# Building the matrix of equal destinations from sign vectors in a two-stage graph network kernel

## The chip, the cores and the metric

The kernel runs as one program on one core of a Trainium2 chip. The metric is the device time of one launch in microseconds, the median of the timed runs. Engine names: PE is TensorE, DVE is VectorE, ACT is ScalarE, POOL is GpSimd, SP is SyncE.

## The reference, cut to what matters

The inputs are 100,000 nodes with 48 features and 25,000 edges, sorted by their destination. Stage one is a gated message pass that sums edge messages into the source nodes, stage two a relational message pass that sums into the destination nodes:

```
h1  = relu(einsum('ni,rij->nrj', h, weight1) + bias1)      # 8 relations
h2  = einsum('nrj,rjo->nro', h1, weight2)
msg = h2[src, rel_type] * norm
agg = segment_sum(msg, dst, num_segments=100000)
x   = x + relu(agg + bias2)
```

Here h is relu(layernorm(x)) after stage one.

## The kernel before

Edges are cut into 49 blocks of 512 (NBLOCK), each block into four tiles of 128 (TILES). Stage one runs over the 49 blocks, then stage two over ROUNDS = 53 rounds, then a closing pass streams 49 chunks of nodes through DVE to the output. All loops are unrolled in Python; each engine has one instruction list that it works through in order, and semaphores tie the lists together.

An indirect add to memory must not meet the same row twice in one transfer. So each block first sums the messages of equal destinations among its own edges: a matrix `same` holds, for tile t, a 1 where the destination of edge i in tiles 0 to t equals that of edge j in tile t and i is not later than j. Ten products per block (`sums_within`, lines 568 to 574) multiply its 128x128 parts with the messages; PE shows two records for each fp32 product. The row sums of `same` (`ahead1`) tell which edge is the last of its kind; `turned1` and `once1` make an index that sends all others to spare rows. POOL then adds four tiles of 128 rows to the table agg1 (`add1`, line 521), and gathers the rows of a block six ahead (`gather_wide`, line 512).

In stage two one round b of the engines' lists works on several blocks:

- DVE (lines 955 to 1063): asum and ac for the block a = b+1 that has just been gathered; v, y, yssq, yvar, yrstd, and three passes over v for x2 (960 elements wide, it also finishes 16 dense rows per partition); stat, cen, evar, erstd for e = b−1; and `same`, `turned1`, `once1` for d = b−2. `same_up_to` (line 854) compares the 512 keys of the block, which SP has broadcast to all 128 partitions (`load_rows1`, line 389), with the keys of one tile, multiplies by the mask `upto` and counts, in four instructions of 128, 256, 384 and 512 columns.
- ACT (lines 717 to 784): copies h2 transposed, scales msg1, squares and relus for block a, the three relus of the hidden layer (hid, 512 wide), the squares sq and ysq, the small square roots astd, estd and ystd, h2, the copy of the sums for POOL, and the copy of the second layer's result.
- PE (lines 620 to 663), for e = b−2 and f = b−3: transposes of h2 and of the messages, the first layer k0, k1, k2 in ps_k[0], ps_k[1], ps_k[0], the block's sums, and the second layer m1.
- POOL: four adds of block b, four gathers of block b+6. An add waits for ACT's copy of the sums and for once1.
- SP: the key rows, the kept values and the dense rows of the round, each after x2 of the round before.

The third set of first-layer products waits for ACT's first relu (line 645), and that stands on ACT behind the square and relu of ac (lines 734 to 742).

Of the kernel before, what the change touches and what calls it, by code (L numbers as in the profile page):

```python
# [7 lines left out]
I32 = mybir.dt.int32  # L8
BF16 = mybir.dt.bfloat16
# [56 lines left out]
POOL_SET = 15  # L66
CONSTS = 13

# [8 lines left out]
def build(nc, table, both, xt_in_dram, xn_in_dram, types, edge_src, edge_dst, src_rows, dst_rows, edge_feat, dist, norm, rel,  # L77
# [13 lines left out]
    with ExitStack() as ctx:  # L91
# [12 lines left out]
        ident = sb("ident", [P, P])  # L104
        iota_rel = sb("iota_rel", [P, NREL])
# [45 lines left out]
        sums1 = ring_of(sb, LAG1, "sums1", [P, TILES, H])  # L151
        junk_l = t2[0][:, :, :].rearrange("p r w -> p (r w)")
# [84 lines left out]
        def psum(name, shape):  # L237
# [14 lines left out]
        ps_h1 = ps_m[0:H, :]  # L252
        ps_gate = ps_s[:, BE // 2:BE // 2 + TILES * H]

        nodes_in = ring_of(sem, ARRIVE, "nodes_in")
# [23 lines left out]
                 "m1t_done msg1_done same1_done turned1_done once1_done sums1_done sums1_copied "  # L279
# [19 lines left out]
        def _(sp):  # L299
# [89 lines left out]
            def load_rows1(b):  # L389
                need(sp, S["same1_done"], b - 1)  # L390
                sp.dma_start(rows[b % 2][:, :], dst_rows[b:b + 1, :].to_broadcast([P, BE])).then_inc(rows_in[b % 2], 16)

            load_rows1(0)
            load_rows1(1)
            for i in range(SKEW, SKEW + T2S):
                load_wide(i)
            for i in range(ROUNDS):
                if 2 <= i < NBLOCK:
                    load_rows1(i)
                sp.wait_ge(S["x2_done"], i + 1)  # L400
                c, j = i - SKEW, i + T2S
                if 0 <= c < NBLOCK - RES:
                    sp.dma_start(x_mid[c], x2[c % 2][:, TILES:G, :].rearrange("p r w -> p (r w)")).then_inc(x_stored[c % 2], 16)
                if SKEW <= j < ROUNDS:
                    load_kept(j)
                    if j >= SKEW + T2S:
                        load_wide(j)
# [20 lines left out]
        def _(pool):  # L428
# [9 lines left out]
            def gather_tile(b, t):  # L438
                s = b % AHEAD
                c = b * TILES + t  # L440
                if t == 0:
# [8 lines left out]
                           allow_small_or_imprecise_dtypes=True).then_inc(S["pool_set"], 1)  # L450
            pool.wait_ge(S["idx_in"], 32)
# [85 lines left out]
        def _(pe):  # L537
# [81 lines left out]
            pe.wait_ge(S["rb1_in"], 2 * 16 * NREL)  # L619
            for b in range(2, NBLOCK + 3):  # L620
# [29 lines left out]
                if f >= 0:  # L650
                    pe.wait_ge(S["same1_done"], f + 1)
# [4 lines left out]
                if e < NBLOCK:  # L656
                    need(pe, S["m1_copied"], e)
# [5 lines left out]
                    last.then_inc(S["m1_done"], 1)  # L663

        @blk.scalar
        def _(act):
# [49 lines left out]

            for b in range(-1, ROUNDS):
# [58 lines left out]
                if 0 <= f < NBLOCK:  # L776
                    act.wait_ge(S["m1_done"], f + 1)
# [14 lines left out]
        def _(dve):  # L792
# [28 lines left out]
            dve.wait_ge(S["pool_set"], POOL_SET + 4)  # L821
            V.tensor_tensor(centre[:, :], centre[:, :], ident[0:2 * H, 0:2 * H], ALU.add).then_inc(S["vec_set"], 1)
# [132 lines left out]
            for b in range(-1, ROUNDS):  # L955
                a, e, d = b + 1, b - 1, b - 2
# [71 lines left out]
                if 0 <= d < NBLOCK:  # L1028
                    dve.wait_ge(S["same1_done"], d + 1)
# [113 lines left out]
```

## Time and profile before

| | us |
|---|---|
| median of 3 timed runs | 1540.43 (1537.09 to 1542.83) |
| span of the profiled execution | 1526.4 |
| stage two, roughly | 755 to 1415 of the span |
| closing pass | 1420 to the end |
| PE, PEld, DVE, ACT, POOL busy | 1130.4, 831.4, 1319.3, 668.1, 1026.1 |

The profile holds the span of the profiled execution, from its first to its last instruction, and no other time of it. Times in the trace count from the span's start. PE is the matmul stream, PEld the weight loads beside it. In a timeline a row merges instructions of one line, with their count behind the x; what stands in brackets is the idle time of the engine before the row and what ended it.

### The profile page before, as it was taken

The numbers are of one execution on the slowest core, as the hardware profiler recorded it, in microseconds if no ns is written. First come the engines' busy times: TensorE is split into PE (matmuls) and PEld (weight loads), VectorE is DVE, ScalarE is ACT, GpSimd is POOL, SyncE is SP. The second block draws the span as 40 slices with busy tenths as digits, with TensorE's granted clock in tenths as the row PEclk, the third lists the DMA queues.
The fourth block names the chain that finished last, engine by engine and source line by source line (L and its number), as shares of the span: only waits on it lengthen the run. The fifth ranks groups of instructions, "written<-read, shape, count | busy, mean of one in ns | idle before, by whom it ended". The sixth has DMA issues, their size and how long they took to land.

```text
span 1526.4 us, 20418 instructions
## 1 busy us (share of the span) xinstructions
PE 1130.4 (74%) x5198; PEld 831.4 (54%) x5198; DVE 1319.3 (86%) x3932; ACT 668.1 (44%) x1627; POOL 1026.1 (67%) x809
## 2 busy tenths in 40 slices
PE   5889899989999899881068888887878887775000
PEld 2767677777777777771035555555555555554000
DVE  6999999999989998980289999998989899888599
ACT  2444444544445444540155555555555555554000
POOL 7655667777877787566667787877777777766000
PEclk9666655655556655655575656655565556666555
DMA  7999986666666656642445666555555555554899
GB/s 225 307 324 327 328 236 157 153 146 143 142 166 149 149 139 143 155 101 11 100 120 143 166 167 156 140 138 137 136 139 127 132 131 138 138 127 81 328 400 398
DMA packets 154391, 268.73 MB, mean 176 GB/s; under 512 B 73818, under 2 KB 90411, under 8 KB 153380
## 3 DMA queue, kind: packets, MB, share of 16 engines
q1 hardware_dynamic: 78228, 223.53, 43.8%
q0 software_dynamic: 68992, 24.64, 18.5%
q10 hardware_dynamic: 7056, 19.27, 3.1%
q8 instruction: 43, 0.70, 0.2%
q14 instruction: 72, 0.59, 0.1%
HBM read 194.33 MB, written 112.55 MB: 201 GB/s over the span
## 4 chain that ended last, share of the span: by engine, by line
PE 34%; DVE 20%; DMA 19%; POOL 12%; issue 10%; ACT 3%; SPq 1%; POOLq 0%; DVEq 0%; ACTq 0%
PE ps_m L572 10%; POOL agg L485 8%; DMA t<-agg,src_all 6%; PE ps_m L661 6%; PE ps_qs L572 6%; DMA lows<-low 4%; PE ps_k L647 3%; DVE same L858 2%; DMA agg<-y,once 2%; DMA agg<-ysq,once 2%; DVE t L1074 2%; DVE x L1070 2%; PE ps_k L559 2%; PE ps_k L560 2%; PE ps_qs L610 1%
## 5 line engine op out<-in xcount | busy, mean ns | idle before, releaser
L521 POOL DMA_INDIRECT agg<-sums,once x196 | 312.7, 1595 | 103.5 <-issue 79.8
L443 POOL DMA_INDIRECT nodes<-in_table,dst_all x196 | 194.9, 995 | 102.2 <-issue 51.7
L512 POOL DMA_INDIRECT t<-agg,src_all x196 | 191.5, 977 | 66.1 <-issue 53.9
L572 PEld LDWEIGHTS ps_m<-msg,same 128*128 128x128 f32 x980 | 200.8, 314 | 29.0 <-issue 29.0
L572 PE MATMUL ps_m<-msg,same 128*128 128x48 f32 x980 | 208.5, 398 | 1.0 <-issue 1.0
L647 PE MATMUL ps_k<-h_t,rw_sb 56*128 56x256 f32 x588 | 122.7, 536 | 114.0 <-ACT hid L742 91.3
L572 PEld LDWEIGHTS ps_qs<-msg,same 128*128 128x128 f32 x980 | 183.6, 289 | 2.1 <-DVE msg L950 2.1
L572 PE MATMUL ps_qs<-msg,same 128*128 128x49 f32 x980 | 180.7, 363 | 2.0 <-DVE msg L950 2.0
L485 POOL DMA_INDIRECT agg<-x,once x84 | 137.4, 1635 | 43.9 <-issue 21.7
L647 PEld LDWEIGHTS ps_k<-h_t,rw_sb 56*128 56x128 f32 x588 | 62.9, 242 | 157.1 <-ACT hid L742 115.2
L559 PE MATMUL ps_k<-types_lo,low_hot 128*128 128x392 bf16 x196 | 95.7, 488 | 52.7 <-DVE low_hot L833 51.0
L661 PE MATMUL ps_m<-hid,rw_sb 128*64 128x256 f32 x588 | 133.8, 625 | 0.0
L973 DVE TENSOR_REDUCE asum<-t 128x4 f32<-128x192 f32 x49 | 17.1, 349 | 114.9 <-DMA t<-agg,src_all 114.8
L839 DVE SCALAR_TENSOR_TENSOR t<-iota_hi,hi_all,ps_k 128x392 f32<-128x392 f32 x196 | 113.8, 617 | 1.5 <-PE ps_k L560 1.5
L858 DVE SCALAR_TENSOR_TENSOR same<-rows,src_all,upto 128x128 f32<-128x128 int32 x196 | 99.8, 546 | 0.0
L485 POOL DMA_INDIRECT agg<-ysq,once x48 | 79.5, 1656 | 29.9 <-DMA agg<-ysq,once 13.8
L485 POOL DMA_INDIRECT agg<-y,once x48 | 77.7, 1619 | 31.9 <-DMA agg<-y,once 16.8
L551 PEld LDWEIGHTS ps_k<-centre,xt 96*128 96x128 f32 x392 | 66.6, 256 | 57.6 <-issue 57.6
L858 DVE SCALAR_TENSOR_TENSOR same<-rows,dst_all,upto 128x128 f32<-128x128 int32 x196 | 96.3, 547 | 0.0
L560 PE MATMUL ps_k<-types_lo,low_hot 128*128 128x392 bf16 x196 | 96.2, 491 | 0.0
L628 PE MATMUL ps_t<-ident,h 128*128 128x128 f32 x98 | 30.0, 404 | 77.3 <-ACT h L774 76.9
L602 PE MATMUL ps_qs<-q_sb,onehot_t 119*128 119x119 f32 x392 | 81.1, 373 | 0.8 <-ACT onehot_t L705 0.8
(149 smaller groups left out, 2620.2 us busy)
## 6 DMA issues: line engine op xcount, KB each, us to landing
agg<-in_both SPq DMA_DIRECT2D x14, 2758.0 KB, 15.3
t<-agg SPq DMA_DIRECT2D x49, 784.0 KB, 5.3
kept<-kept_out SPq DMA_DIRECT2D x49, 404.0 KB
kept_in<-kept SPq DMA_DIRECT2D x49, 404.0 KB, 3.5
agg<-bias_rows SPq DMA_DIRECT2D x49, 384.0 KB
out<-t ACTq DMA_DIRECT2D x49, 384.0 KB, 5.8
rows<-in_src_rows SPq DMA_DIRECT2D x49, 256.0 KB, 4.2
rows<-in_dst_rows SPq DMA_DIRECT2D x49, 256.0 KB, 3.2
```

Source lines behind the costliest of these rows:

```text
L443: pool.indirect_dma_start(nodes[s][:, t, :], None, table, bass.IndirectOffsetOnAxis(ap=dst_all[:, c:c + 1], axis=0)).then_inc(nodes_in[b % ...
L485: pool.indirect_dma_start(agg0, bass.IndirectOffsetOnAxis(ap=once[b % LAG][:, t:t + 1], axis=0), sums[b % LAG][:, t, :], None, compute_op= ...
L512: pool.indirect_dma_start(t2[b % T2S][:, t, :], None, wide, bass.IndirectOffsetOnAxis(ap=src_all[:, c:c + 1], axis=0)).then_inc(ends_in[b ...
L521: pool.indirect_dma_start(agg1, bass.IndirectOffsetOnAxis(ap=once1[b % LAG1][:, t:t + 1], axis=0), sums1[b % LAG1][:, t, :], None, compute ...
L559: mm(ps_l[t % 2], low_hot[:, 0, t * P:(t + 1) * P], types_lo[:, 0, :], start=True, stop=False)
L560: mm(ps_l[t % 2], low_hot[:, 1, t * P:(t + 1) * P], types_lo[:, 1, :], start=False, stop=True).then_inc(S["low_done"], 1)
L572: last = mm(ps[:, t * width:(t + 1) * width], kept_same[:, at:at + P], m[:, v, :], start=(v == t), stop=(v == TILES - 1))
L602: last = mm(ps_q[:, t * NTYPE:(t + 1) * NTYPE], onehot_t[:, t * P:(t + 1) * P], q_sb[:, :], start=True, stop=True)
L647: last = mm(ps_k[k % 2][:, h, 0:BE // 2], rw1_sb[HALF * h:HALF * h + H + NREL, k * P:(k + 1) * P], h2_t[HALF * h:HALF * h + H + NREL, :], ...
L661: last = mm(ps_m[HALF * h:HALF * (h + 1), 0:BE // 2], rw2_sb[:, k, :], hid1[:, k, h, :], start=(k == 0), stop=(k == KC - 1))
L839: V.scalar_tensor_tensor(out=junk_l[:, t * NHI:(t + 1) * NHI], in0=iota_hi[:, :], scalar=hi_all[:, c:c + 1], in1=ps_l[t % 2], op0=ALU.is_e ...
L858: last = V.scalar_tensor_tensor(out=same[b % 2][:, at:at + n], in0=rows[b % 2][:, 0:n], scalar=keys[:, b * TILES + t:b * TILES + t + 1], i ...
```

## The change

In stage two the matrix `same` no longer comes from compares on DVE. SP loads the keys of four blocks at once, each broadcast to 32 partitions (`load_keys`). In every fourth round DVE shifts them by the partition's number and keeps one bit, and one round later turns the bits into +1 and −1 in bf16 (`signs`, which lie where `upto` was; stage one no longer needs it). For each tile PE multiplies the 32 sign rows of the tile's edges with those of all edges up to it; equal keys give 32, others at most 30. A second product with the identity adds −64 where the edge in the tile's own 128x128 part is later. ACT writes relu(product − 31) to `same`, and its accumulator gives `ahead1`. The products use ps_k[1]: tiles 0 and 1 in one part of its first half, tile 2 in the second half, tile 3 in the first half once tiles 0 and 1 are read. DVE's `turned1` and `once1` move one round later (d = b−3).

```diff
-POOL_SET = 15
+POOL_SET = 16
+GROUP = 4
+NBITS = 32
+GROUPS = -(-NBLOCK // GROUP)
+APART = -2.0 * NBITS
...
+        signs = [upto[:, :].bitcast(BF16)[:, k * BE:(k + 1) * BE] for k in range(2)]
+        ps_dots = [ps_k[1][:, 0, 0:P], ps_k[1][:, 0, P:3 * P], ps_k[1][:, 1, 0:3 * P], ps_k[1][:, 0, 0:BE]]
...
@@ SP
-            def load_rows1(b):
-                need(sp, S["same1_done"], b - 1)
-                sp.dma_start(rows[b % 2][:, :], dst_rows[b:b + 1, :].to_broadcast([P, BE])).then_inc(rows_in[b % 2], 16)
+            def load_keys(k):
+                need(sp, S["signs_done"], k - 1)
+                for q in range(GROUP):
+                    b = min(k * GROUP + q, NBLOCK - 1)
+                    sp.dma_start(rows[k % 2][q * NBITS:(q + 1) * NBITS, :],
+                                 dst_rows[b:b + 1, :].to_broadcast([NBITS, BE])).then_inc(keys_in[k % 2], 16)
...
-                if 2 <= i < NBLOCK:
-                    load_rows1(i)
+                if i % GROUP == 2 and 2 <= i // GROUP + 2 < GROUPS:
+                    load_keys(i // GROUP + 2)
@@ PE
+            def key_dots(b, t):
+                at = slice(b % GROUP * NBITS, (b % GROUP + 1) * NBITS)
+                bits = signs[b // GROUP % 2]
+                mm(ps_dots[t], bits[at, t * P:(t + 1) * P], bits[at, 0:(t + 1) * P], start=True, stop=False)
+                mm(ps_dots[t][:, t * P:(t + 1) * P], ident_bf[:, :], later[:, :], start=False, stop=True).then_inc(S["dots_done"], 1)
...
                         if k == 1:
-                            need(pe, S["relu1_done"], e)
+                            need(pe, S["same1_done"], TILES * e)
...
                     sums_within(ps_sums1, H, same[f % 2], msg1).then_inc(S["sums1_done"], 1)
                 if e < NBLOCK:
+                    pe.wait_ge(S["signs_done"], e // GROUP + 1)
+                    pe.wait_ge(S["relu1_done"], e + 1)
+                    for t in range(TILES - 1):
+                        key_dots(e, t)
                     need(pe, S["m1_copied"], e)
...
                     last.then_inc(S["m1_done"], 1)
+                    pe.wait_ge(S["same1_done"], TILES * e + 2)
+                    key_dots(e, TILES - 1)
@@ ACT
+            def same1_copy(b, t):
+                act.wait_ge(S["dots_done"], b * TILES + max(t + 1, 2))
...
+                A(same[b % 2][:, place(t):place(t) + n], ps_dots[t], ACT.Relu, bias=1.0 - NBITS,
+                  accum_out=ahead1[:, t:t + 1]).then_inc(S["same1_done"], 1)
...
                     A(ysq[:, r, :], y[:, r, :], ACT.Square).then_inc(S["ysq_done"], 1)
+                if 0 <= f < NBLOCK:
+                    same1_copy(f, 0)
+                    same1_copy(f, 1)
                 if a < NBLOCK:
                     act.wait_ge(S["avar_done"], a + 1)
...
                     last.then_inc(S["h2_done"], 1)
                 if 0 <= f < NBLOCK:
+                    same1_copy(f, 2)
                     act.wait_ge(S["m1_done"], f + 1)
...
                     nc.scalar.copy(msg1_t[:, :], ps_m[:, 0:BE // 2]).then_inc(S["m1_copied"], 1)
+                    same1_copy(f, 3)
@@ DVE
+            V.tensor_copy(ident_bf[:, :], ident[:, :])
+            V.tensor_scalar(bit_of[:, :], bit_of[:, :], NBITS - 1, None, ALU.bitwise_and)
+            V.tensor_scalar(later[:, :], upto[:, BE - P:BE], -APART, APART, ALU.mult, ALU.add)
...
-                a, e, d = b + 1, b - 1, b - 2
+                a, e, d = b + 1, b - 1, b - 3
...
-                if 0 <= d < NBLOCK:
-                    dve.wait_ge(rows_in[d % 2], 16 * (uses(NBLOCK - 1 - d % 2, 2) + uses(d, 2)))
-                    need(dve, S["sums1_done"], d - 1)
-                    same_up_to(d, dst_all, ahead1).then_inc(S["same1_done"], 1)
+                if 0 <= b < NBLOCK + GROUP - 1 and b % GROUP == 1:
+                    dve.wait_ge(S["bits_done"], b // GROUP + 1)
+                    V.tensor_scalar(signs[b // GROUP % 2], rows[b // GROUP % 2][:, :], 2.0, -1.0, ALU.mult,
+                                    ALU.add).then_inc(S["signs_done"], 1)
...
+                if 0 <= b < NBLOCK and b % GROUP == 0:
+                    k = b // GROUP
+                    dve.wait_ge(keys_in[k % 2], 16 * GROUP * uses(k, 2))
+                    need(dve, S["dots_done"], GROUP * TILES * (k - 1))
+                    V.tensor_scalar(rows[k % 2][:, :], rows[k % 2][:, :], bit_of[:, :], 1, ALU.logical_shift_right,
+                                    ALU.bitwise_and).then_inc(S["bits_done"], 1)
```

## Rows read from the trace of the kernel before

**Rows 1.** The page's busy times: engine, us, share of the span, instructions

```profile
PE 1130.4 (74%) x5198; PEld 831.4 (54%) x5198; DVE 1319.3 (86%) x3932; ACT 668.1 (44%) x1627; POOL 1026.1 (67%) x809
```

**Rows 2.** Windows: length; PE, PEld, DVE, ACT, POOL busy (instructions); clock; DMA share, GB/s

```profile
790.00:1350.00 560.00, 451.02 (x2016) 307.40 (x2016) 510.77 (x1346) 297.04 (x882) 435.06 (x339) 0.60 0.57 142
40.00:680.00 640.00, 587.65 (x2735) 460.82 (x2734) 596.34 (x2118) 306.09 (x565) 451.23 (x342) 0.62 0.74 193
```

**Rows 3.** Waits, 1020 to 1290 us: who <- releaser: total us, times, longest

```profile
PE ps_k L647 <- ACT hid L742: 41.3, 17, 5.1
...
DVE asum L973 <- DMA t<-agg,src_all: 21.4, 10, 2.5
```

**Rows 4.** Timeline of POOL: start, us, engine, line, what, [idle before]

```profile
1099.65 1.60 POOL L521 DMA_INDIRECT agg<-sums,once  x1 [1.68 <-issue]
...
1111.10 0.94 POOL L512 DMA_INDIRECT t<-agg,src_all  x1 [0.30 <-issue]
1112.34 1.61 POOL L521 DMA_INDIRECT agg<-sums,once  x1 [0.30 <-issue]
...
1126.33 1.61 POOL L521 DMA_INDIRECT agg<-sums,once  x1 [1.68 <-issue]
```

**Rows 5.** Timeline of DVE in the same two rounds

```profile
1115.25 0.35 DVE L990 SCALAR_TENSOR_TENSOR ac<-asum,t 128x192 f32<-128x192 f32 x1
...
1118.02 0.34 DVE L858 SCALAR_TENSOR_TENSOR same<-rows,dst_all,upto 128x128 f32<-128x128 int32 x1
...
1119.90 0.35 DVE L1018 TENSOR_REDUCE kept_in<-asq 128x4 f32<-128x192 f32 x1
...
1127.47 0.34 DVE L990 SCALAR_TENSOR_TENSOR ac<-asum,t 128x192 f32<-128x192 f32 x1
```

**Rows 6.** Timeline of ACT in the same rounds

```profile
1120.81 0.30 ACT L765 ACTIVATE estd<-evar,eps 128x4 f32<-128x4 f32 x1 [0.22 <-DVE evar L1024]
1122.08 0.31 ACT L769 ACTIVATE ystd<-yvar,eps_sq 128x20 f32<-128x20 f32 x1 [0.98 <-DVE yvar L1037]
...
1125.25 0.32 ACT L781 COPY sums<-ps_m 128x192 f32<-128x192 f32 x1 [1.80 <-PE ps_m L661]
```

**Rows 7.** Timeline of PE: a round at full clock, then rounds near 1100

```profile
784.06 0.70 PE L647 MATMUL ps_k<-h_t,rw_sb 56*128 56x256 f32 x4 [0.63 <-ACT hid L742]
784.69 2.43 PE L572 MATMUL ps_m<-msg,same 128*128 128x48 f32 x20
787.05 1.42 PE L661 MATMUL ps_m<-hid,rw_sb 128*64 128x256 f32 x6
...
1091.26 4.50 PE L572 MATMUL ps_m<-msg,same 128*128 128x48 f32 x20
...
1103.47 4.50 PE L572 MATMUL ps_m<-msg,same 128*128 128x48 f32 x20
1107.90 2.83 PE L661 MATMUL ps_m<-hid,rw_sb 128*64 128x256 f32 x12
...
1116.79 1.22 PE L647 MATMUL ps_k<-h_t,rw_sb 56*128 56x256 f32 x4 [3.31 <-ACT hid L742]
1117.94 4.50 PE L572 MATMUL ps_m<-msg,same 128*128 128x48 f32 x20
```

**Rows 8.** Timeline of PE in stage one, at a granted clock of 0.50

```profile
412.03 0.53 PE L559 MATMUL ps_k<-types_lo,low_hot 128*128 128x392 bf16 x1
412.35 0.53 PE L560 MATMUL ps_k<-types_lo,low_hot 128*128 128x392 bf16 x1
412.82 1.94 PE L610 MATMUL ps_qs<-w2b_sb,gate_in 49*128 49x48 f32 x8
```

**Rows 9.** Lines of 780 to 1420 us, then whole run: busy us, mean ns

```profile
L749 ACT ACTIVATE hid<-ps_k 128x512 f32<-128x512 f32 x47 | 27.3, 581 | 0.0
...
L725 ACT COPY h_t<-ps_t 128x256 f32<-128x256 f32 x47 | 17.5, 372 | 30.2 <-PE ps_t L635 30.2
...
L802 DVE TENSOR_SCALAR t<-t 49x512 int32<-49x512 int32 x1 | 0.4, 419 | 3.7 <-DMA t<-in_src_rows 3.7
```

More of the change, by code:

```diff
@@ L65 @@
 RES = 38
-POOL_SET = 15
+POOL_SET = 16
 CONSTS = 13
+GROUP = 4
+NBITS = 32
+assert GROUP * NBITS == P
+GROUPS = -(-NBLOCK // GROUP)
+APART = -2.0 * NBITS
 def place(t):
@@ L104, in build @@
         ident = sb("ident", [P, P])
+        ident_bf = sb("ident_bf", [P, P], BF16)
+        later = sb("later", [P, P], BF16)
+        bit_of = sb("bit_of", [P, 1], I32)
         iota_rel = sb("iota_rel", [P, NREL])
@@ L252, in build @@
         ps_h1 = ps_m[0:H, :]
+        ps_dots = [ps_k[1][:, 0, 0:P], ps_k[1][:, 0, P:3 * P], ps_k[1][:, 1, 0:3 * P], ps_k[1][:, 0, 0:BE]]
         ps_gate = ps_s[:, BE // 2:BE // 2 + TILES * H]
+        keys_in = pair_of(sem, "keys_in")
         nodes_in = ring_of(sem, ARRIVE, "nodes_in")
@@ L278, in build @@
                  "h2_done h2t_done h2t_copied k0_done k1_done k2_done relu0_done relu1_done relu2_done m1_done m1_copied "
-                 "m1t_done msg1_done same1_done turned1_done once1_done sums1_done sums1_copied "
+                 "m1t_done msg1_done bits_done signs_done dots_done same1_done turned1_done once1_done sums1_done sums1_copied "
                  "x_beta_done out_done").split()
@@ L387, in load_kept @@
                 sp.dma_start(kept_in[s][:, TILES * H:TILES * H + KEPT], kept[i - SKEW]).then_inc(kept_got[s], 16)
-            def load_rows1(b):
-                need(sp, S["same1_done"], b - 1)
-                sp.dma_start(rows[b % 2][:, :], dst_rows[b:b + 1, :].to_broadcast([P, BE])).then_inc(rows_in[b % 2], 16)
-            load_rows1(0)
-            load_rows1(1)
+            def load_keys(k):
[4 more added lines that the diff above has]
+                                 dst_rows[b:b + 1, :].to_broadcast([NBITS, BE])).then_inc(keys_in[k % 2], 16)
+            load_keys(0)
+            load_keys(1)
             for i in range(SKEW, SKEW + T2S):
@@ L450, in _ @@
                            allow_small_or_imprecise_dtypes=True).then_inc(S["pool_set"], 1)
+            nc.gpsimd.iota(bit_of[:, :], pattern=[[0, 1]], base=0, channel_multiplier=1).then_inc(S["pool_set"], 1)
             pool.wait_ge(S["idx_in"], 32)
@@ L650, in _ @@
                 if f >= 0:
-                    pe.wait_ge(S["same1_done"], f + 1)
+                    pe.wait_ge(S["same1_done"], TILES * (f + 1))
                     pe.wait_ge(S["msg1_done"], f + 1)
@@ L715, in _ @@
             sums0_copy(NBLOCK - 1)
+            def same1_copy(b, t):
+                act.wait_ge(S["dots_done"], b * TILES + max(t + 1, 2))
+                if t == 0:
+                    need(act, S["sums1_done"], b - 1)
+                    need(act, S["turned1_done"], b)
+                n = P * (t + 1)
+                A(same[b % 2][:, place(t):place(t) + n], ps_dots[t], ACT.Relu, bias=1.0 - NBITS,
+                  accum_out=ahead1[:, t:t + 1]).then_inc(S["same1_done"], 1)
             for b in range(-1, ROUNDS):
@@ L1028, in _ @@
                 if 0 <= d < NBLOCK:
-                    dve.wait_ge(S["same1_done"], d + 1)
+                    dve.wait_ge(S["same1_done"], TILES * (d + 1))
                     V.scalar_tensor_tensor(out=turned1[:, :], in0=ahead1[:, :], scalar=1.0, in1=turn1_all[:, d * TILES:(d + 1) * TILES],
                                            op0=ALU.is_gt, op1=ALU.mult).then_inc(S["turned1_done"], 1)
+                if 0 <= b < NBLOCK and b % GROUP == 0:
[4 more added lines that the diff above has]
+                                    ALU.bitwise_and).then_inc(S["bits_done"], 1)
                 if yes:
```

## The prediction

> **What bounds the kernel now.** I read the page first. VectorE (DVE) is the busiest engine, 86% of the span [rows 1], but that is a mean over a first stage, a second and a closing transfer, and the edit touches the second alone. So next the table by windows: in 560 us of stage two DVE is busy 91%, TensorE (PE) 81%, GpSimd (POOL) 78% and ScalarE (ACT) 53% [rows 2]. POOL shows 339 instructions there, eight to a round, so 42.4 rounds, 13.21 us each. With three engines that close, the busy share decides nothing. I looked in the list of waits for what each sits idle on: DVE waits only for the landing of gathered rows, 10 times in 270 us, and PE only for ACT's first eviction of the hidden layer [rows 3]. Those waits alternate, and four cycles explain them, all from the timelines of rounds near 1100 us:
>
> - POOL by itself: four scatter-adds and four gathers, 1099.65 to 1112.34, 12.69 us [rows 4].
> - DVE by itself: ac at 1115.25 to ac at 1127.47, 12.22 us [rows 5].
> - PE by itself, without a long wait: one block's sums at 1091.26, the next at 1103.47, 12.21 us [rows 7].
> - Gathers through all engines, two rounds long. POOL's adds start at 1099.65, its last gather at 1111.10, ac follows at 1115.25, the last first-layer products at 1116.79, the sums at 1117.94, ACT's copy of the sums at 1125.25, and that frees POOL's next idle start at 1126.33 [rows 4 to 7]. Together 26.68 us, 13.34 a round: this is the one that binds, and it agrees with the mean of 13.21.
>
> The reader should see that the compares (1118.02 to 1119.90 on DVE [rows 5]) lie in the DVE cycle, which has 1 us to spare, and not in the cycle through the gathers.
>
> **The change part by part.** *DVE loses* the four compares, 1.88 us a round [rows 5]. It gains two 128x512 instructions in four rounds. The nearest row is a 512-wide integer operation on 49 partitions, 0.419 us [rows 9]: 0.2 us a round, between 0.1 and 0.4 if each cost half or twice that. The DVE cycle falls to some 10.5 us. That saves nothing directly, since 12.22 was not the bound.
>
> *PE gains*, per block, four products of 32 rows and four corrections of 128 rows: 128+256+384+512 and 4x128 columns, 1792 in all. Two bf16 products of 392 columns (line 560) start 0.32 apart (392 columns at 1.2 GHz are 0.327); I take 1792 columns as 1.49 us at that level. From such a product to one that uses another part of the array (line 610) the step is 0.47, so the change of shape costs 0.14 [rows 8]. The new products alternate 32 and 128 rows: seven changes more per block, 0.98. Together 2.47 us at the low clock; bounds 1.5 (no changes of shape) and 3.3 (weight loads uncovered as well, by 0.1 each). The PE cycle becomes 14.68 at the low clock.
>
> *ACT gains* four evictions. A 256-wide copy takes 0.372 and a 512-wide relu 0.581 [rows 9], so 128, 256, 384 and 512 wide are 0.27, 0.37, 0.48 and 0.58: 1.7 us. What an accumulated sum costs on ACT no row shows; below, 0 (its idle tail overlaps the next), above, 0.2 each, one more small operation. ACT's load rises to under 9 us of a round and stays covered. The places matter more than the load.
>
> *The new wait.* The first two evictions stand between ACT's square of y and its three small square roots, and wait for the first two products, which PE issues only behind the sums of the previous block. Queued behind that wait on ACT are the three roots, h2, the copy of the sums. DVE waits for the roots (erstd, yrstd) and then has three passes over y, x2 and the next round's ac. And ac gates, through ACT, the next round's last first-layer products, which stand ahead of the sums. That closes a cycle of one round that did not exist:
>
> - ac to last first-layer products 1116.79 − 1115.25 = 1.54, to the sums 1.15 [rows 5, 7];
> - the sums, 1103.47 to 1107.90, 4.43 [rows 7];
> - two products with corrections, 640 columns 0.53 and four changes 0.56: 1.09;
> - two evictions, 0.27+0.37 and a little for the sums: 0.70 (0.46 to 1.1);
> - three roots back to back, 0.30 and 0.31 by their rows, less overlap: 0.80 [rows 6];
> - end of the last root 1122.39 to the next ac 1127.47: 5.08 [rows 5, 6].
>
> Sum 14.79 us at the low clock. The DVE time that the change frees lies in front of the roots, where DVE now waits.
>
> *The clock.* Rows show the sums at either level: 4.43 at 0.5 and 784.69 to 787.05, 2.36, at full; the four products before them 1.15 and 0.63 [rows 7]. The PE part of the cycle, 6.67, would be 3.54 at full. Stage two had a mean of 0.60 and stage one, where PE is busy 92%, 0.62 [rows 2]: a fifth of the time at full. A fifth at a rate 1.88 times as high makes 6.67 into 5.67, and the cycle 13.79. I take 0.60, as the fuller stage one has hardly more.
> The Trainium skill, "TensorE: Matmul & The Clock Gate", section "Why this matters for your kernels", says that TensorE should be kept busy without gaps to hold its full clock. By that rule the change, which fills PE's gaps, would bring 2.4 GHz. Against it stands stage one's 0.62 at 92%; by the row I sum with 0.60.
>
> *The gather cycle* gets longer too: the copy of the sums waits for the second layer, and three products now stand ahead of that: 1152 columns 0.96 and six changes 0.84. 28.48 over two rounds, 14.24 at the low clock, some 13.5 with a fifth at full. It lies just under the new cycle and will take over in some rounds. I take 13.85 a round.
>
> *Moved and hidden.* turned and once go one round later: POOL's add needs the copy of the sums of that same round anyway, and once comes ahead of it. The key rows come as 52 issues of 64 KB, four in every fourth round, in place of 49 of 256 KB: SP's queue spends its rounds waiting for x2, so the extra issues fit there, and 9 MB fewer move. The fourth product waits for evictions done 2 us earlier (the second layer, 2.83 us, covers it [rows 7]), and the fourth eviction lies beside PE's transposes. If that cover went, ACT's copy of h2 would be late by about 0.5 a round. Four setup instructions: at most 1 us.
>
> *Sum.* (13.85 − 13.21) x 42.4 = 27 us. In the last three blocks there are no gathers and PE sets the pace: 2.47/1.18 x 3 = 6. With setup 1: 34 us. The span was 1526.4, the median of the timed runs 1540.43, 14.0 above, which I leave as it is (the profile gives no other time of its own execution). So 1526.4 + 34 + 14 = 1574 us.
>
> **The rivals.** *PE's clock stays low* (1615 us): the new cycle runs at 14.79, since the short full stretches have fallen beside the sums till now: 4.50 long in nearly all rounds near 1100 us. 1.58 x 42.4 + 7 + 1 = 75. For it: those rows; against it: PE loses the gaps that they were tied to.
>
> *Nothing to measure* (1543): changes of shape cost nothing in a 32-row product and the evictions overlap: 0.60 and 0.50 in place of 1.09 and 0.70 make 14.10, with a fifth at full 13.17; −2 for the rounds, +5 for end and setup. For it: ACT's tails overlap elsewhere; against it: the step in [rows 8].
>
> *PE at full clock* (1519, faster): the new cycle falls to 1.54+0.63+2.36+0.55+0.70+0.80+5.08 = 11.66, the gather cycle under 12.7, and POOL's 12.69 bounds. (12.69 − 13.21) x 42.4 = −22, with +1 for the end. By 8.12 + 6.67/(1 + 0.88 s) the cycle is under 13.21 from a share s of 0.35 at full, and short enough to be told from no change from 0.46. Against it speaks stage one. The rule of the Trainium skill named above speaks for it.
>
> *The change does not do what it says*, in that DVE still bounds: excluded by the DVE cycle of 10.5.
>
> **How the numbers follow.** The forecast, a new one-round cycle at the usual mix of clocks, 0.53; its own range is 1550 to 1600 (evictions 0.46 to 1.1, changes of shape 0.07 to 0.2). Low clock 0.17; nothing to measure 0.13; full clock or cheap products 0.17. About 0.5%, 8 us, is what a measurement can tell from no change. Faster 0.17, same 0.13, slower 0.70. The range 1520 to 1612 leaves out half of the full-clock case and the worse half of the low-clock one.
>
> **What would show it.** In the profile after: ACT idle ahead of the first eviction, released by PE's products, some 3 us a round; DVE idle ahead of erstd and yrstd, released by ACT's roots, and no longer ahead of asum; rounds of 13.5 to 14.8 without the alternation of 12.2 and 14.5; PE's 32-row products at steps over columns/1.2 GHz by 0.14. PE's new work under 1.6 us a block would refute the changes of shape. Sums at 2.4 us in most rounds, a granted clock over 0.75 and POOL without gaps would refute the forecast for the fast rival; DVE idle still mostly ahead of asum would mean that the gather cycle stayed the bound.

## The result and the profile after

The changed kernel takes 1585.68 us (median of 4 runs, 1578.58 to 1591.63), the kernel before 1538.76 us (4 runs, 1525.08 to 1542.83): a ratio of 1.0325, 95% interval 1.0275 to 1.0375. It is slower, by 47 us. The forecast was slower, 1574 us in a range of 1520 to 1612.

The profiled execution took 1585.55 us, its span is 1583.7. Against the span of before that is 57.3 us more. DVE's first ac of stage two starts at 766.27 in place of 753.09 us. Of those 13 us 10.4 lie ahead of the first block's sums in stage one, which start at 49.90 in place of 39.48 us, though stage one's code is the same but for a few short setup instructions. The profile of before is the odd one here: in the twelve kernels below, none of which changes stage one either, these sums start between 46.6 and 50.6, and the first ac of stage two between 753.3 and 767.0. (With the change it lies at 760.5 to 767.0, without it at 753.1 to 760.6, so a few us may still belong to the change; no run tests that.) The 48 rounds from the first ac to the last take 648.4 us in place of 604.1, so the change costs 44.3 there. The rest, up to the end, is 0.2 shorter. The loss is one microsecond in each round.

The busy times of the page after, and the window of 560 us that answers to [rows 2]:

```profile
PE 1224.0 (77%) x5590; PEld 867.6 (55%) x5590; DVE 1244.3 (79%) x3569; ACT 740.0 (47%) x2019; POOL 1024.0 (65%) x810
...
790.00:1350.00 560.00, 491.24 (x2209) 314.82 (x2209) 411.65 (x963) 335.22 (x1136) 401.94 (x312) 0.60 0.48 117
```

POOL's 312 instructions, eight to a round, are 39 rounds where [rows 2] had 42.4. DVE's work per round fell from 12.0 to 10.6 us and PE's grew from 10.6 to 12.6; the busiest, PE, stands at 88% of the window, so something waits. The list of waits, 1020 to 1290 us (total us, times, longest), says what:

```profile
ACT same L750 <- PE ps_k L639: 70.3, 22, 3.9
DVE erstd L1095 <- ACT estd L804: 52.4, 17, 3.4
...
PE ps_k L668 <- ACT hid L778: 26.3, 19, 2.0
...
DVE asum L1017 <- DMA t<-agg,src_all: 0.2, 1, 0.2
```

In [rows 3] DVE lost 21.4 us to the gathered rows. That is gone; it now waits 52.4 us ahead of erstd, and ACT waits 70.3 us ahead of an eviction (the instruction that takes a product's result to `same`) for PE's new products. The round from 1113.67 us on shows the whole ring, as I call the prediction's new one-round cycle. First DVE (columns as in [rows 4]):

```profile
1113.67 0.35 DVE L1034 SCALAR_TENSOR_TENSOR ac<-asum,t 128x192 f32<-128x192 f32 x1
...
1123.01 0.18 DVE L1095 RECIPROCAL erstd<-estd 128x4 f32<-128x4 f32 x1 [3.36 <-issue]
...
1128.28 0.35 DVE L1034 SCALAR_TENSOR_TENSOR ac<-asum,t 128x192 f32<-128x192 f32 x1
```

Then PE:

```profile
1115.21 1.23 PE L668 MATMUL ps_k<-h_t,rw_sb 56*128 56x256 f32 x4 [1.91 <-ACT hid L778]
1116.36 4.50 PE L587 MATMUL ps_m<-msg,same 128*128 128x48 f32 x20
1120.80 0.28 PE L638 MATMUL ps_k<-upto 32*128 32x128 bf16 x1
1121.01 0.29 PE L639 MATMUL ps_k<-later,ident_bf 128*128 128x128 bf16 x1
1121.23 0.39 PE L638 MATMUL ps_k<-upto 32*128 32x256 bf16 x1
1121.55 0.29 PE L639 MATMUL ps_k<-later,ident_bf 128*128 128x128 bf16 x1
1121.77 0.50 PE L638 MATMUL ps_k<-upto 32*128 32x384 bf16 x1
...
1122.41 2.68 PE L686 MATMUL ps_m<-hid,rw_sb 128*64 128x256 f32 x12
```

And ACT:

```profile
1121.87 0.28 ACT L750 ACTIVATE same<-ps_k 128x128 f32<-128x128 f32 x1 [3.90 <-PE ps_k L639]
1122.05 0.19 ACT L750 ACTIVATION_READ_ACCUMULATOR same<-ps_k 128x1 f32 x1
1122.14 0.38 ACT L750 ACTIVATE same<-ps_k 128x256 f32<-128x256 f32 x1
1122.40 0.20 ACT L750 ACTIVATION_READ_ACCUMULATOR same<-ps_k 128x1 f32 x1
1122.49 0.29 ACT L799 ACTIVATE kept_in<-kept_in,eps 128x4 f32<-128x4 f32 x1
...
1122.87 0.30 ACT L808 ACTIVATE ystd<-yvar,eps_sq 128x20 f32<-128x20 f32 x1
```

Read in order of time: ac, 1.54 later the last first-layer products, 1.15 later the sums, 4.44 later the first new product, 1.07 later ACT's first eviction, 0.62 for two evictions with their counts, 0.68 for three roots, 5.11 to the next ac. Together 14.61 us, where the prediction had 14.79 for this ring at the low clock.

Of the 40 rounds from the seventh block on the mean is 14.28 us (before 13.21). They are 14.0 to 14.7 but for five of 12.9 to 13.0. The alternation of 12.2 and 14.5 is gone.

### The profile page after: what moved, and what is told of

Read it like the earlier page. It is cut to its first block, busy times and chain, and to the rows that moved or that the text cites. A ratio compares the mean times of both kernels' runs of the same rounds, so it can differ in the third digit from the quotient of the medians.

```text
span 1583.7 us, 21296 instructions
## 1 busy us (share of the span) xinstructions
PE 1224.0 (77%) x5590; PEld 867.6 (55%) x5590; DVE 1244.3 (79%) x3569; ACT 740.0 (47%) x2019; POOL 1024.0 (65%) x810
## 4 chain that ended last, share of the span: by engine, by line
PE 33%; DVE 30%; issue 12%; POOL 9%; DMA 8%; ACT 6%; SPq 1%; another core or an unknown queue 0%; ACTq 0%; DVEq 0%; POOLq 0%
PE ps_m L587 11%; POOL agg L500 8%; PE ps_qs L587 5%; DVE ps_qs L1106 4%; DVE ps_qs L1104 4%; PE ps_k L668 3%; DVE x_res L1110 3%; DMA agg<-x,once 2%; DVE x L1120 2%; DVE t L1124 2%; DVE t L883 2%; PE ps_qs L625 2%; PE ps_qs L617 2%; PE ps_k L574 2%; PE ps_k L575 2%
## 5 line engine op out<-in xcount | busy, mean ns | idle before, releaser
L527 POOL DMA_INDIRECT t<-agg,src_all x196 | 190.0, 970 | 68.5 <-issue 52.4
L587 PEld LDWEIGHTS ps_m<-msg,same 128*128 128x128 f32 x980 | 195.8, 307 | 27.9 <-issue 26.5
L587 PE MATMUL ps_m<-msg,same 128*128 128x48 f32 x980 | 203.5, 391 | 1.2 <-ACT same L750 1.2
L668 PE MATMUL ps_k<-h_t,rw_sb 56*128 56x256 f32 x588 | 119.2, 521 | 81.1 <-ACT hid L778 55.6
L750 ACT ACTIVATE same<-ps_k 128x128 f32<-128x128 f32 x196 | 83.7, 430 | 174.9 <-PE ps_k L639 168.9
L686 PE MATMUL ps_m<-hid,rw_sb 128*64 128x256 f32 x588 | 137.5, 639 | 0.0
L1095 DVE RECIPROCAL erstd<-estd 128x4 f32<-128x4 f32 x49 | 8.7, 178 | 140.4 <-ACT estd L804 128.4
L566 PEld LDWEIGHTS ps_k<-centre,xt 96*128 96x128 f32 x392 | 70.0, 268 | 61.7 <-issue 61.7
L500 POOL DMA_INDIRECT agg<-y,once x48 | 78.2, 1628 | 29.7 <-issue 12.6
L686 PEld LDWEIGHTS ps_m<-hid,rw_sb 128*64 128x64 f32 x588 | 60.6, 220 | 42.5 <-issue 36.8
```

What stands on the lines that cost most here:

```text
L500: pool.indirect_dma_start(agg0, bass.IndirectOffsetOnAxis(ap=once[b % LAG][:, t:t + 1], axis=0), sums[b % LAG][:, t, :], None, compute_op= ...
L527: pool.indirect_dma_start(t2[b % T2S][:, t, :], None, wide, bass.IndirectOffsetOnAxis(ap=src_all[:, c:c + 1], axis=0)).then_inc(ends_in[b ...
L587: last = mm(ps[:, t * width:(t + 1) * width], kept_same[:, at:at + P], m[:, v, :], start=(v == t), stop=(v == TILES - 1))
L668: last = mm(ps_k[k % 2][:, h, 0:BE // 2], rw1_sb[HALF * h:HALF * h + H + NREL, k * P:(k + 1) * P], h2_t[HALF * h:HALF * h + H + NREL, :], ...
L686: last = mm(ps_m[HALF * h:HALF * (h + 1), 0:BE // 2], rw2_sb[:, k, :], hid1[:, k, h, :], start=(k == 0), stop=(k == KC - 1))
```

## The experiments

Each kernel ran beside runs of the kernel before, whose median was 1531.1 to 1542.7 us; so ratios to it are compared, with their 95% intervals. Two ratios less than half a per cent apart cannot be told from each other. "Rounds" are means over the same 40 rounds of each trace. Times of rounds are from ac to ac.

### PE's work without the new wait: load_only, dots_first, evict_late

**load_only**: the kernel before, with the new products beside its compares; nobody reads them.

```diff
+                    pe.wait_ge(S["relu1_done"], e + 1)
+                    for t in range(TILES - 1):
+                        key_dots(e, t)      # behind the sums, ahead of the second layer
...
+                    key_dots(e, TILES - 1)
```

> The kernel before, with compares on DVE, and on PE in addition the same products per block (32-row and 128-row, 1792 columns) at the same places, read by nobody: no eviction, no new wait for ACT or DVE. Theory: without the wait on ACT there is no new cycle, but the gather cycle takes the three products (1.61 us at the low clock) once in two rounds: 14.0 to 14.15 a round against 13.21, so 1571 to 1580; DVE idle ahead of asum, and longer than before. Rival (only the new wait costs, PE's work is covered): 13.2 to 13.4 a round, 1536 to 1548. Rival (PE's throughput): 14.5 a round, 1590 or more.

Measured: 1633.41 us, ratio 1.0628 [1.0571, 1.0684], rounds 15.08. A miss: PE's work alone costs more than the whole change. The second rival's time (1590 or more) came, but not for its reason: PE still waits 36.4 us in 270 for ACT's first relu, up to 6.8 at a time, so its throughput is not the limit. The rounds alternate between 12.2 and 16.4 to 19.5 us (18.0 in the mean). In one long round (POOL's last gather; SyncE's issue of the 784 KB load of dense rows; DVE's asum):

```profile
1108.29 0.94 POOL L512 DMA_INDIRECT t<-agg,src_all  x1 [0.30 <-issue]
...
1108.22 0.43 SPq L382 DMA_DIRECT2D t<-agg  x1
...
1113.98 0.35 DVE L985 TENSOR_REDUCE asum<-t 128x4 f32<-128x192 f32 x1 [5.73 <-DMA t<-agg,src_all]
```

From the last gather to asum it is 5.7 us. In the kernel before it was 3.4: the last gather at 1111.10 [rows 4], then

```profile
1112.27 0.43 SPq L382 DMA_DIRECT2D t<-agg  x1
...
1114.50 0.35 DVE L973 TENSOR_REDUCE asum<-t 128x4 f32<-128x192 f32 x1 [2.19 <-DMA t<-agg,src_all]
```

so that the load went out 1.2 us after the gather. Thus the gather cycle became longer than the prediction's 28.48 for two rounds, and I formed a second theory: the gathered rows land late because of that load. (The kept rows' load, 404 KB, goes out 0.4 us ahead of it each time.)

**dots_first**: the changed kernel, but PE runs a block's first three new products ahead of the sums of the block before, so ACT's evictions no longer wait for those sums.

```diff
                 if e < NBLOCK:
+                    pe.wait_ge(S["signs_done"], e // GROUP + 1)
+                    pe.wait_ge(S["relu1_done"], e + 1)
+                    for t in range(TILES - 1):
+                        key_dots(e, t)
...                  # the sums of block f follow; the same four lines behind them go
```

> The changed kernel with the first three products of a block issued ahead of the previous block's sums on PE, no longer behind them; all work is the same. Theory (the new one-round cycle products, evictions, roots, x2, ac, last first-layer products, sums is what binds at 14.54 us): the cycle loses the 4.4 us of the sums and no longer binds; the gather cycle, 26.68 + 1.61 over two rounds, 14.15 a round, and PE's own 14.5 at the low clock stand just behind, so the mean round falls from 14.28 only to 13.6 to 14.15, 5 to 28 us off the changed kernel's 1586, and DVE's idle time moves from erstd back to asum. Rival (PE's load alone binds): mean round 14.28 as it is, 1580 to 1592, PE without idle time. Rival (ACT's evictions as such cost): no change either, DVE still waits at erstd.

Measured: 1610.91 us, ratio 1.0453 [1.0398, 1.0508], rounds 14.71. A miss too. The new ring is gone (DVE waits 10.0 us for the roots in 270, not 52.4), but DVE waits 43.7 us for gathered rows, up to 5.7 at a time, in rounds mostly of 12.0 and of 16 to 19. ACT's evictions have a wait of their own in this order, 24.7 us for DVE's `turned1`, at most 1.4 at a time.

**evict_late**: the changed kernel with one edit on ACT; the first two evictions move from ahead of the three roots to behind h2. PE's order stays.

```diff
                 if 0 <= f < NBLOCK:
-                    same1_copy(f, 0)
-                    same1_copy(f, 1)
...                  # three roots, h2
+                    same1_copy(f, 0)
+                    same1_copy(f, 1)
                     same1_copy(f, 2)
```

> The changed kernel with one edit on ACT: the first two evictions of a block stand behind h2, not ahead of the three roots. PE's order is the changed kernel's. Theory: this takes the new one-round cycle away (DVE idle ahead of erstd 52.4 us in 270 falls under 15), and the gather cycle, which PE's new products lengthen too, takes over with its alternation of short and long rounds: 14.2 to 15.1 us a round, 1578 to 1622 us, so not faster than the changed kernel (1586). Rival: the new wait is the whole loss; then the rounds fall to 13.2 to 13.5 and the time to 1535 to 1555.

Measured: 1623.63 us, ratio 1.0554 [1.0513, 1.0596], rounds 14.85. As expected by the theory, with a time 1.6 us above its range. Its waits, 1020 to 1290 us, in place of the four lines above:

```profile
POOL agg L536 <- issue: 57.6, 73, 5.0
DVE asum L1016 <- DMA t<-agg,src_all: 55.5, 16, 5.7
...
ACT same L750 <- PE ps_k L639: 19.0, 22, 1.1
```

No wait of DVE for the roots is left in the list, and by the two ratios the kernel is 2.2% slower than the changed one. The wait sets the changed kernel's pace, yet taking it away alone makes things worse.

### The load beside the gathers: dots_wide_late, evict_wide_late, wide_late, change_wide_late, early_wide_late

One edit on SyncE in all five: the loads of the dense rows and of the kept rows go out only once asum, which reads the gathered rows, is done.

```diff
                 if SKEW <= j < ROUNDS:
+                    if j >= SKEW + T2S:
+                        sp.wait_ge(S["asum_done"], min(i + 3, NBLOCK))
                     load_kept(j)
```

> The kernel dots_first (the first three products of a block ahead of the sums of the block before, so that the new one-round cycle is gone) with one edit on SyncE: in stage two the 784 KB load of dense rows waits until the next round's asum is done, so that it no longer goes out within a microsecond of a block's last gather. Theory: dots_first is slow (14.7 us a round, 1610.9 us, pairs of 12.0 and 18.1) because the gathered rows land behind that load, 5.4 us after the last gather in place of 3.4. Then DVE's longest idle time ahead of asum falls from 5.7 to under 4 us, a pair of rounds from 30.2 to 28.0 to 28.8, the mean round to 14.0 to 14.4, and the time to 1575 to 1598. Rival 1: the landing is late for another reason; then the mean round stays at 14.7 and the time within 1603 to 1620. Rival 2: the dense rows, loaded later, are themselves late for x2; then DVE idles ahead of x2 and the time is above 1620.

Measured: 1566.52 us, ratio 1.0222 [1.0158, 1.0286], rounds 13.68: 1.0 us a round less than dots_first. The direction is the theory's, but the gain is larger than its range (14.0 to 14.4). Last gather, asum, and the load behind it:

```profile
1109.42 0.95 POOL L529 DMA_INDIRECT t<-agg,src_all  x1 [0.30 <-issue]
...
1111.85 0.35 DVE L1020 TENSOR_REDUCE asum<-t 128x4 f32<-128x192 f32 x1 [0.43 <-DMA t<-agg,src_all]
...
1112.65 0.43 SPq L393 DMA_DIRECT2D t<-agg  x1
```

It is 2.4 us from gather to asum without the load, against 5.4 in dots_first (gather at 1107.33, load at 1107.68, asum at 1112.75). The edit holds back the kept rows' load as well; which of the two loads costs the time was not separated.

> The kernel evict_late with the 784 KB load of dense rows held back until the next round's asum. Theory: as dots_first gained 0.023 in its ratio to the kernel before by that edit (1.0453 to 1.0222; rounds 14.7 to 13.7 us), so does this one: rounds 13.5 to 14.0, ratio 1.010 to 1.027 (1547 to 1578 us), and faster than the changed kernel with both of its costs (the wait of the roots and the load beside the gathers) gone; what is left is the longer gather cycle at PE's low clock. Rival: the load is not what costs here: ratio as in evict_late, within 0.6%.

Measured: 1566.93 us, ratio 1.0187 [1.0124, 1.0251], rounds 13.80. As expected: with the wait for the roots gone and the loads away from the gathers the kernel gains 1.3% on the changed one. Still it loses 1.9% to the kernel before, and DVE still waits for the gathered rows (44.4 us in 270, at most 3.6).

> The kernel before with the same edit on SyncE alone. In the profile of before the 784 KB load goes out 1.2 us after a block's last gather, which landed 3.4 us after its issue. Theory: the load still shares the engines with those gathers, so the landing shortens by 0.3 to 1 us per pair of rounds, the mean round falls from 13.21 to 12.9 to 13.1, and the time by 5 to 15 us (1525 to 1538). Rival 1: before, the load came behind the gathers and cost nothing: no change, 1535 to 1546. Rival 2: the load comes late for x2 of the next round: slower, above 1550.

Measured: 1524.05 us, ratio 0.9939 [0.9906, 0.9972], rounds 12.90. As expected: 7 us less than its own runs of before, though the time is 1 us below the range. Beside evict_wide_late it seems to price PE's work in the gather cycle free of the load: 13.80 − 12.90 = 0.90 us a round, and the prediction's two sums for that cycle, 28.48 and 26.68 over two rounds, differ by 0.90 a round too. But the agreement is in part luck. In wide_late POOL waits at most 0.5 us at a time, 28.1 us in 84 waits, nearly all of it the 0.3 that stands between any two of its instructions; so POOL's pace and not the gather cycle sets the 12.90. And PE's clock differs: the sums last 4.39 us in wide_late and 3.71 in evict_wide_late.

> The changed kernel with the 784 KB load held back alone. Theory: its rounds are set by the new one-round cycle (DVE waited for the gathered rows for 0.2 us in 270), so the edit gains nothing: ratio to the kernel before 1.027 to 1.038, rounds 14.1 to 14.4. Rival: the load costs in the changed kernel as in dots_first: ratio under 1.020.

Measured: 1591.07 us, ratio 1.0328 [1.0283, 1.0373], rounds 14.21. As expected: the same edit gains nothing where the new ring sets the pace. In the changed kernel, from 900 to 1300 us, the load goes out 2.3 us or more behind the last gather in each round.

> The kernel sums_early (1521.97 us, ratio 0.989; 12.87 us a round, with 0.6 us idle ahead of asum in nearly each) with the same edit on SyncE. Theory: POOL's own 12.69 us is the bound that is left and the idle time at asum belongs to the landing; that goes, the round falls to 12.69 to 12.80 and the time by 3 to 8 us (1513 to 1520). Rival: POOL bounds already and the idle time at asum is only DVE waiting for POOL: no change (1519 to 1526). If the dense rows come late: slower, above 1530.

Measured: 1520.91 us, ratio 0.9936 [0.9904, 0.9969], rounds 12.90. A miss: no gain on sums_early (0.9891, below), as the rival said. POOL has no idle time there but 0.3 between instructions; DVE's short waits at asum, 11.5 us in 270 and at most 0.8, cost nothing then.

### The clock and the price of the products: fill, no_corr

**fill**: the changed kernel with two more products of 256 columns a block, read by nobody, where PE waits for ACT's first eviction of the hidden layer.

```diff
+                            if f >= 0:
+                                for _ in range(2):
+                                    mm(ps_m[:, 0:BE // 2], rw1_sb[0:H + NREL, 0:P], h2_t[0:H + NREL, :], start=True, stop=True)
```

> The changed kernel with two more fp32 products of 256 columns on PE (1.7 us at the low clock, results overwritten) in the gap in which PE waits for ACT's first relu. Theory (the granted clock is low in the sums because it rises only late in an unbroken run of PE and each round's gap breaks the run): with the gap filled full stretches reach the sums more often, mean clock in them 0.6 or more against 0.525, and rounds get shorter than 14.28 in spite of more work: 13.6 to 14.2, 1560 to 1583. Rival (the place of the full stretches does not hang on the gap): clock in the sums as before, rounds 14.28 to 14.7, 1586 to 1604.

Measured: 1566.08 us, ratio 1.0177 [1.0123, 1.0232], rounds 13.73. As the theory expected: PE got more to do and the kernel became about 20 us faster. Its sums last 3.50 us in the mean, those of the changed kernel 4.35; the trace has 4.50 for the sums at a granted clock of 0.50 and 2.43 at 1.00. Its window (clock: last figure but two):

```profile
790.00:1350.00 560.00, 507.48 (x2433) 326.86 (x2432) 429.05 (x994) 346.23 (x1185) 414.86 (x322) 0.66 0.49 121
```

**no_corr**: the changed kernel without the corrections.

```diff
-                mm(ps_dots[t], bits[at, t * P:(t + 1) * P], bits[at, 0:(t + 1) * P], start=True, stop=False)
-                mm(ps_dots[t][:, t * P:(t + 1) * P], ident_bf[:, :], later[:, :], start=False, stop=True).then_inc(S["dots_done"], 1)
+                mm(ps_dots[t], bits[at, t * P:(t + 1) * P], bits[at, 0:(t + 1) * P], start=True, stop=True).then_inc(S["dots_done"], 1)
```

> The changed kernel without the four corrections on PE (the products that mark which of two equal destinations comes later are left out, so each count takes in all edges): per block 512 columns and all changes between products of 32 and 128 rows but those at the two ends less. Theory: two of the four corrections, 256 columns (0.21 us) and three changes of shape at the measured 0.11, stand in the new cycle, 0.54 us a round at the low clock; rounds from 14.28 to 13.65 to 13.95, 12 to 27 us less, 1559 to 1574 (ratio 1.013 to 1.023). Rival 1: a change of shape costs nothing there: 0.21 a round, 1575 to 1580. Rival 2: PE's clock turns with the load that is taken off, as it rose when load was put on (fill): sums at 4.5 us in every round, or at 2.4 in a good part of them; then the time leaves this range, and the granted clock in the sums leaves 0.50 to 0.60.

Measured: 1568.52 us, ratio 1.0196 [1.0158, 1.0234], rounds 13.74, sums 4.29. As the theory expected: the rounds at the low clock (the median of the 40) fall from 14.54 to 14.00, by the 0.54 of two products of 128 columns and three changes of shape. Its three products, with no change between them:

```profile
1106.99 0.81 PE L638 MATMUL ps_k<-upto 32*128 32x128 bf16 x3
1107.73 0.69 PE L685 MATMUL ps_m<-hid,rw_sb 128*64 128x256 f32 x1
```

From the first start to the second layer it is 0.74 us for 768 columns, 0.64 at 1.2 GHz: 0.10 more once, where the changed kernel has 0.11 behind each product.

### The way out: sums_early, change_early

**sums_early**: the kernel before; PE runs the sums of the block before between the second and the third part of the first layer, not behind it, and ACT moves its copy of the sums ahead of h2 and the third relu behind it.

```diff
                         if k == 2:
+                            if f >= 0:
+                                block_sums(f)
...
-                if f >= 0:
+                if f >= 0 and e == NBLOCK:
+                    block_sums(f)
```

> The kernel before with the order of PE and ACT changed: the block's sums stand between the second and the third set of first-layer products instead of behind the third, ACT copies them behind its small roots and takes the third relu later. Theory (the gather cycle binds the kernel before, since the sums wait behind products that wait for ac): the copy of the sums comes 2.9 us or more earlier in a round that waits for gathers, the cycle falls to 23.8 over two rounds, POOL's own 12.69 binds: rounds of 12.7 to 12.9, 1516 to 1528, DVE no longer idle ahead of asum. Rival (DVE or PE binds the kernel before as such): 13.2 a round and 1535 to 1545, or more where the third relu comes too late for the second layer.

Measured: 1521.97 us, ratio 0.9891 [0.9836, 0.9946], rounds 12.87. As expected: DVE's wait for gathered rows falls from 21.4 us, up to 2.5 [rows 3], to 12.3 us, up to 0.7. This shows that the gather cycle bound the kernel before; the shorter landing in wide_late speaks for the same.

**change_early**: the changed kernel in the same order on PE, with its first two evictions behind h2. On ACT:

```diff
                 if 0 <= f < NBLOCK:
-                    same1_copy(f, 0)
-                    same1_copy(f, 1)
...                  # three roots; ACT's copy of the sums comes here now; h2
+                    act.wait_ge(S["k2_done"], f + 1)
+                    A(hid1[:, 2, :, :], ps_k[0][:, :, 0:BE // 2], ACT.Relu).then_inc(S["relu2_done"], 1)
+                    same1_copy(f, 0)
+                    same1_copy(f, 1)
                     same1_copy(f, 2)
```

> The changed kernel with the order of sums_early: PE runs a block's sums between the two halves of the next block's first layer instead of behind them, so the sums come before the new products need PE; ACT copies the sums before the roots, and takes the first three evictions and the third relu behind h2. This shortens both cycles at once, the one through the gathers and the new one through the roots. What is left is PE's own work, 14.5 us a round if all at 1.2 GHz and under 11 at 2.4 GHz. Theory: PE now bounds itself without waits, its clock decides: a round of 13.3 to 14.0 us at the usual mean of 0.60 to 0.63 and 1545 to 1575 us, faster than the changed kernel (1586) by 10 to 40 and still behind the kernel before (1540) or level with it; DVE idle ahead of erstd under 1 us a round. Rival 1: PE's clock in the sums stays at 1.2 GHz as in the changed kernel (0.525 there): 14.5 a round, 1585 to 1595. Rival 2: with PE never waiting, its clock rises: under 13.0 a round, 1515 to 1535.

Measured: 1517.88 us, ratio 0.9891 [0.9826, 0.9957], rounds 12.70. A miss on the fast side; rival 2 had the time. The window of [rows 2] and two waits:

```profile
790.00:1350.00 560.00, 490.89 (x2484) 310.07 (x2480) 467.26 (x1078) 373.87 (x1285) 450.31 (x350) 0.68 0.52 131
...
POOL agg L536 <- issue: 26.5, 87, 0.3
...
DVE asum L1022 <- DMA t<-agg,src_all: 14.6, 8, 5.4
```

POOL makes 350 instructions, 43.75 rounds, and never waits over 0.3 us: its own 12.69 us [rows 4] binds, and the change neither costs nor gains anything any more. PE is as busy as in the changed kernel, 491 us, and has done 12% more rounds, at a clock of 0.68. Rival 2 gave as its reason that PE would never wait; that did not hold, since PE waits 1.7 us ahead of the second layer in the round near 1090 us. What raised its clock is not settled. This kernel and sums_early have the lowest ratios of the study, equal within their intervals; those of wide_late and early_wide_late overlap with them.

## Why the prediction was right, and where it was off

**The bound before** was named rightly (sums_early). So was **what the change removes**: DVE's compares were no part of that bound, and DVE's work of a round came to 10.6 us where 10.5 was said for its cycle.

**PE's gain.** From one new product to the next the trace has 0.21 us for 128 columns and 0.32 for 256 at the low clock, that is the columns at 1.2 GHz and 0.11 more. So the change of shape costs 0.11 and not 0.14: some 2.3 us a block for a forecast of 2.47. The weight loads of the same products show what it consists of:

```profile
1120.79 0.10 PEld L638 LDWEIGHTS ps_k<-upto 32*128 32x128 bf16 x1
1121.01 0.10 PEld L639 LDWEIGHTS ps_k<-later,ident_bf 128*128 128x128 bf16 x1
1121.22 0.10 PEld L638 LDWEIGHTS ps_k<-upto 32*128 32x128 bf16 x1
```

Each load starts with its own product, behind the columns of the product before, and lasts the 0.10 that is lost; in no_corr the three loads of 32 rows lie beside one another and are paid once. The prediction's upper bound had counted the change and an uncovered weight load as two prices.

**The new ring** is there as it was put, with DVE late at erstd and ACT at its first eviction; term by term it is 14.61 for 14.79. The evictions (0.62 for 0.70) and the roots (0.68 for 0.80) were a little dear.

**The clock** is the step that failed. I took the mean of 0.60, "a fifth of the time at full", for the PE part of the ring and made 14.79 into 13.79 and, with the gather cycle, 13.85. The mean was right: 0.60 in the window. But it does not hold for that part. The granted clock (last figure but two) in the changed kernel over two rounds, first from about the sums' start to the end of the third new product, then from there to the next ac. The third row is from the round between them, 6.20 us from about its sums' start:

```profile
1088.26:1094.46 6.20, 6.20 (x29) 4.84 (x25) 3.46 (x9) 2.05 (x4) 5.06 (x4) 0.50 0.53 106
1094.46:1100.66 6.20, 5.47 (x28) 2.55 (x27) 5.08 (x13) 4.90 (x22) 3.51 (x3) 0.76 0.16 29
...
1103.35:1109.55 6.20, 6.20 (x34) 4.33 (x34) 4.42 (x13) 3.75 (x14) 4.98 (x5) 0.58 0.45 72
...
1116.36:1122.41 6.05, 6.05 (x28) 4.94 (x26) 2.58 (x8) 2.02 (x6) 4.83 (x5) 0.50 0.55 96
1122.41:1128.28 5.87, 4.95 (x27) 2.44 (x26) 5.14 (x13) 4.51 (x20) 3.00 (x4) 0.80 0.14 24
```

In these rounds the full level came only after PE had worked without a long break since its wait ahead of the third part of the first layer (1115.21 above), that is in the second layer and the transposes, which lie beside the ring. When the next sums come, behind another wait, it is gone in most rounds; in the round between it still reached the start of the sums. It does not come in each round: from 1141.87 to 1182.83 us the level is half throughout, though PE has no break of over 0.5 us there from 1142.78 on. What decides that is not settled. The sums average 4.35 us, so by 4.50 at half and 2.43 at full only (4.50 − 4.35)/2.07 = 7% of them ran at full, where the forecast had put a fifth. The rounds became 14.28 and not 13.85: 0.43 × 42.4 = 18 us too few. The rows were there before: in [rows 7] the sums near 1100 us are 4.50 long in each round. That was the rival at the low clock, given 0.17; the truth, 14.28, lies between its 14.79 and the forecast, and by its reason it is the rival's: most rounds run at the low-clock 14.5. fill shows the same the other way round: shift where the full level falls and 20 us come back. The Trainium skill, "TensorE: Matmul & The Clock Gate", section "Why this matters for your kernels", would have TensorE kept busy without gaps. The trace agrees for fill, whose filled gap raised the clock in the window to 0.66. It disagrees for the change, which raised PE's busy time from 451 to 491 us and left the clock at 0.60, and for no_corr, which brought it back to 451 us and shows 0.65. Nor does the window's mean price the ring: in no_corr the sums still last 4.29 us.

**The gather cycle** was said to lie just under the new ring. With the dense load as it was, it lay above it: 14.7 to 15.1 us a round in the three kernels without the long wait for the roots. Whether its lengthening by PE (0.90) was sized well is not shown, for the reason given at wide_late. The landing was taken over from [rows 4, 5] unchanged, though it grows once the load goes out beside the last gather.

**The sums around it.** The tail of 6 us did not come (−0.2); which cover it had was not tested. The 14.0 us between the span and the median are no time outside the span: the profiled execution of after lies 1.9 above its span. What I carried over was mostly the scatter between executions that shows ahead of stage one's first sums (39.48 us in the profile of before). That the time came within 12 us of 1574 is in part luck: from the first ac to the end the kernel is 44.1 us longer for a forecast of 33, the 18 us of the clock set against the 6 of the tail; the 13 us of stage one nearly took the place of the 14. The setup cost 0.3 for 1, by the start of stage one's first products on PE (18.46 for 18.12 us).

## What to carry to other kernels

A work item moved to a less busy engine can close a ring through that engine's queue: list what stands behind each new wait and follow it to the wait's own cause. Where PE's clock has two levels, a term on the path takes the level of its own rows, not the stage's mean. And a wait that shows in the trace may shield something worse: before taking it away, look for the next cycle and the transfers that would move; here an order on PE and ACT in which the sums come early mended both cycles at once.

## What was not expected of the hardware

- A block's gathered rows were read by asum 2.4 us after the start of its last gather with no large load beside them, 3.4 with a 784 KB load issued 1.2 us behind, 5.4 to 5.7 with it issued within 0.4 us. Over 900 to 1300 us it is 2.4 to 2.9 in dots_wide_late, 3.0 to 3.7 at 1.2 us in before, and 5.4 to 6.0 in the rounds of dots_first with the load 0.2 to 0.4 us behind.
- Work added to PE's gap made the kernel 20 us faster (fill): more of its sums fell into stretches at full clock.
- A change between products of 32 and of 128 rows costs about the same at both levels of the clock. At half it is 0.11 us; in change_early, where the clock was full, the step from a product of 128 columns to the next is 0.15 us (946.57 to 946.72), 0.05 of it columns at 2.4 GHz and 0.10 the change; the weight loads there last 0.09 to 0.10 us. The prediction's sums at full clock had halved it.
- The read of ACT's accumulator is an instruction of 0.19 to 0.20 us, but the eviction that stands behind it starts only 0.09 us after it did (1122.05 and 1122.14 above).
